# A three-pass attention and expert kernel on one core: GpSimd in place of VectorE for sixteen subtractions

## The reference, cut to what matters

```python
x = x + tanh(g_xattn[0]) * _L0_xattn_ref(..., _layernorm(x), ctx_2048)   # a recurrence (wkv)
x = x + tanh(g_ffn[0]) * _L0_ffn_ref(_layernorm(x), ...)                 # ternary weights, 8-bit tokens
x = x + tanh(g_xattn[1]) * _L1_xattn_ref(_layernorm(x), ctx_2048, ...)   # attention, 32 heads of 8
x = x + tanh(g_ffn[1]) * _L1_ffn_ref(_layernorm(x), ...)                 # 64 experts, top 8, one shared
```

```python
q = _rmsnorm(q)
k = _rmsnorm(k)
scores = jnp.einsum('bhnd,bhmd->bhnm', q, k) * scale
attn = jax.nn.softmax(scores, axis=-1)
```

## Time and profile before

| what | value |
|---|---|
| median of 3 runs | 480.92 us (478.32 to 481.01) |
| the profiled execution's own time | 480.34 us |
| its span in the trace | 478.6 us |
| mean granted TensorE clock | 0.963 of full speed |
| TensorE, matmuls: busy | 399.1 us (83%) |
| VectorE busy | 379.5 us (79%) |
| ScalarE busy | 302.0 us (63%) |
| GpSimd busy | 0.2 us |

### The profile page before, as it was taken

How to read it: one execution, slowest core, us unless ns; L and a number is a source line. 1 busy time by engine, 2 the same in 40 slices (tenths; PEclk the granted TensorE clock), 3 DMA queues, 4 the chain that set the end, 5 groups by cost and what they waited for, 6 DMA issues and landing times.

```text
span 478.6 us, 7806 instructions
## 1 busy us (share of the span) xinstructions
PE 399.1 (83%) x2612; PEld 193.7 (40%) x2612; DVE 379.5 (79%) x817; ACT 302.0 (63%) x442; POOL 0.2 (0%) x4
## 2 busy tenths in 40 slices
PE   1011966697776897999999999999999999999996
PEld 1010444342424454554534443554444444444443
DVE  5999499999998869999797898897456666777754
ACT  5896686689696766757898677464234444444422
POOL 0000000000000000000000000000000000000000
PEclk9999999577898899999999999999999999999999
DMA  8500200000002164114425336244222655556511
GB/s 295 223 1 0 66 1 1 1 1 0 2 2 66 46 213 128 56 57 121 140 72 159 119 111 195 80 143 131 87 66 73 209 164 167 167 172 175 174 38 44
DMA packets 31506, 47.47 MB, mean 99 GB/s; under 512 B 5610, under 2 KB 15210, under 8 KB 30956
## 3 DMA queue, kind: packets, MB, share of 16 engines
q1 hardware_dynamic: 31468, 46.98, 31.4%
HBM read 45.65 MB, written 1.31 MB: 98 GB/s over the span
## 4 chain that ended last, share of the span: by engine, by line
PE 61%; DVE 22%; ACT 7%; issue 4%; DMA 3%; SPq 2%; DVEq 0%; ACTq 0%
PE ps L1593 31%; PE ps L1927 15%; PE ps L1702 5%; PE ps L1690 2%; DVE xn L1034 1%; DVE bn L1015 1%; DMA regC<-in_ctxT_dram 1%; DVE rep L1163 1%; DVE regW L1483 1%; PE ps L1618 1%; DMA regP<-in_dp_dram 1%; PE ps L1584 1%; ACT exs L723 1%; SPq L538 1%; PE ps L1712 1%
## 5 line engine op out<-in xcount | busy, mean ns | idle before, releaser
L934 ACT ACTIVATE regW<-ps 128x512 f32<-128x512 f32 x51 | 30.4, 597 | 92.6 <-PE ps L1593 89.7
L1593 PE MATMUL ps<-hH,regC 128*128 128x512 f16 x264 | 85.8, 380 | 0.1
L1500 DVE TENSOR_TENSOR regW<-ps,regW 128x512 f32<-128x512 f32 x64 | 44.1, 690 | 51.8 <-PE ps L1593 49.0
L1593 PE MATMUL ps<-hH,regW 128*128 128x512 f16 x248 | 80.9, 383 | 0.2 <-DVE regW L1500 0.2
L1593 PE MATMUL ps<-hL,regC 128*128 128x512 f16 x132 | 50.0, 379 | 0.0
L1927 PE MATMUL ps<-regW,regC 128*128 128x512 f16 x198 | 48.1, 379 | 0.0
L1593 PE MATMUL ps<-hL,regW 128*128 128x512 f16 x124 | 47.4, 382 | 0.0
L1927 PE MATMUL ps<-regW 128*128 128x512 f16 x180 | 43.8, 379 | 3.4 <-DVE regW L1483 3.4
L1483 DVE TENSOR_TENSOR regW<-regW 128x512 f16<-128x512 f32 x64 | 43.6, 681 | 0.1
L947 ACT CAST regW<-regW 128x512 f16<-128x512 f32 x64 | 39.2, 612 | 0.6 <-DVE regW L1521 0.5
L1593 PEld LDWEIGHTS ps<-hH,regC 128*128 128x128 f16 x264 | 25.8, 98 | 32.6 <-issue 3.6
(11 more groups left out here) (202 smaller groups left out, 662.1 us busy)
## 6 DMA issues: line engine op xcount, KB each, us to landing
regW<-routing_dram SPq DMA_DIRECT2D x130, 128.0 KB, 3.1
regP<-in_gu_dram SPq DMA_DIRECT2D x56, 256.0 KB, 2.6
regP<-in_dp_dram SPq DMA_DIRECT2D x56, 128.0 KB, 2.7
regO<-in_ffn_dram SPq DMA_DIRECT2D x3, 1024.0 KB, 9.4
x<-in_x_dram SPq DMA_DIRECT2D x2, 512.0 KB, 8.3
regC<-in_ctxT_dram SPq DMA_DIRECT2D x1, 1024.0 KB, 5.3
regP<-in_proj_dram SPq DMA_DIRECT2D x1, 768.0 KB, 12.2
out_dram<-x SPq DMA_DIRECT2D x1, 512.0 KB, 3.5
```

Source lines behind the costliest of these rows:

```text
L934: nc.scalar.activation(sgm[:, c % 2, :], bank(gate_bank(c)), ACT.Silu, scale=UNSCALE).then_inc(esilu_done, 1)
L1500: V.tensor_tensor(rows, bank(gate_bank(c) + 1), rows, ALU.mult).then_inc(et_done, 1)
L1593: mm = T.matmul(out_ap, w(k), a(k), start=(n == 0), stop=(n == 3 * DK - 1))
```

## The change

The function `split_low` moves from VectorE's part of the program to a new part of GpSimd, with the same operands, the same wait and the same semaphore at its end. GpSimd calls it for n = 0 to 15 in a row. On VectorE the ten calls in the plain list and the six in the table of the products are gone, and the calls around them close up. The lists of the other engines are as they were.

```diff
-            (6, "C"): [("ffn_residual", 7, 7), ("split_low", 10), ("split_low", 11), ("stats", 9)],
+            (6, "C"): [("ffn_residual", 7, 7), ("stats", 9)],
...
-            (11, "C"): [("split_low", 12), ("low_halves", 9, 7), ("heads_sum", 16, 6), ("split_low", 13),
-                ("weights_low", 13)],
+            (11, "C"): [("low_halves", 9, 7), ("heads_sum", 16, 6), ("weights_low", 13)],
...
-            (14, "C"): [("split_low", 14), ("split_low", 15), ("weights_low", 16), ("weights_low", 17),
+            (14, "C"): [("weights_low", 16), ("weights_low", 17),
...
-                V.tensor_tensor(lo, src, hi, ALU.subtract).then_inc(repL, 1)
...
+        @block.gpsimd
+        def _(pool):
+            def split_low(n):
+                pool.wait_ge(repH, n + 1)
+                R = rep[:, n % 2]
+                src = kc[:, n % HT, :].rearrange("p (h d) -> p h d", h=HEADS).unsqueeze(2).broadcast_to([P, HEADS, 2, HD])
+                hi, lo = (R[:, :, 0:4:2, :], R[:, :, 1:4:2, :]) if of_keys(n // 2) else (R[:, :, 0:2, :], R[:, :, 2:4, :])
+                nc.gpsimd.tensor_tensor(lo, src, hi, ALU.subtract).then_inc(repL, 1)
+
+
+            for n in range(2 * TT):
+                split_low(n)
```

More of the change, by code:

```diff
@@ L1364, in _ @@
             rows_begin(1)
-            split_low(0)
-            split_low(1)
             rows_end(1)
@@ L1370, in _ @@
             row_sums(2)
-            split_low(2)
-            split_low(3)
             ffn_residual(3, 6)
@@ L1380, in _ @@
             running_max(2)
-            split_low(4)
             low_halves(4, 3)
-            split_low(5)
             turned_rows(4, 1)
@@ L1400, in _ @@
             heads_sum(6, 3)
-            split_low(6)
-            split_low(7)
             heads_sum(7, 2)
@@ L1425, in _ @@
             weights_low(0)
-            split_low(8)
-            split_low(9)
             heads_out(2, 4)
@@ L1459, in beside @@
                         rows(*at)
-                    elif name == "split_low":
-                        split_low(*at)
                     elif name == "stats":
```

## The result

The changed kernel takes 483.13 us (median of 20 runs, 479.39 to 484.7) where the kernel before takes 480.48 us in the same series (20 runs, 478.24 to 482.37). The ratio is 1.0047, with a 95% interval of 1.0029 to 1.0064: half a per cent slower, or 2.3 us. It lies 2.1 us above the forecast of 481.0 and within 0.3 us of rival 1 (483.4). The profiled execution of the changed kernel is the shortest of its 20 runs (479.39 us, span 477.6), so its span says nothing about the 2.3 us. Only its shifts between one place and the next can be read.

What follows compares the result with a forecast made beforehand. From 200 us TensorE was taken to bound the kernel, earlier the hand-overs among VectorE, ScalarE and TensorE. Terms -0.47 + 1.09 - 0.57 = +0.05 us on 480.34 gave 480.4, with 0.6 for the median 481.0; range 478.0 to 487.0.

Steps and rivals of the forecast that it cites:

- rival 1: VectorE and GpSimd hold each other up over SBUF operands, mainly at tiles 4 and 5: +2.4 us, 483.4; chance 0.33.
- The price d: Time of one moved subtraction on GpSimd: taken as 1.22 us, with ends 0.68 and 2.29.
- Term A: Tiles 0 to 3: the second copy of turned tiles ends earlier, -0.47 us.
- Term B: Tiles 6 and 7: TensorE turns tile 7 late and nothing covers it, so the scores come late, +1.09 us.
- Pair (4,5): Tiles 4 and 5: covered by ScalarE's and TensorE's work, earlier gain carried on; no term in the sum.
- term C: Tiles 8 and 9: VectorE, relieved, has the variance 1.2 us earlier, then ScalarE's own queue is late: -0.57 us.
- TensorE's clock: Risk of both signs: a gap in TensorE's work at another place could add or take 2 us.
- Tiles 10 to 15: Beside the products, from 200 us, where TensorE is busy 99.6%: the products cover the move, costed at nothing.

Runs made afterwards that it cites:

- e10: Against the kernel before, only the subtractions of tiles 6 and 7 moved to GpSimd: 481.14 us against 480.54, ratio 1.0012.
- e9: Against the kernel before, only the subtractions of tiles 4 and 5 moved to GpSimd: 482.94 us against 480.35, ratio 1.0057.
- e3: The change with tiles 4 and 5 back on VectorE: 480.16 us against 480.63 for the kernel before, ratio 0.9994.
- e6: Kernel before, nothing moved; GpSimd adds two unneeded two-operand subtractions behind each upper half: 487.36 us against 480.35, ratio 1.0153.
- e7: Kernel before, nothing moved; GpSimd adds two unneeded zero writes behind each upper half: 480.59 us against 480.35, ratio 1.0010.
- e12: The change with TensorE turning tile 5 ahead of group 1's weighted values: 480.94 us against 480.54 for the kernel before, ratio 1.0011.
- e1: The change, all sixteen on GpSimd, with a semaphore of their own: 483.02 us against 480.63 for the kernel before, ratio 1.0040.
- e2: The change with tiles 6 and 7 back on VectorE: 482.46 us against 480.63 for the kernel before, ratio 1.0043.
- e4: Against the kernel before, only tiles 0 to 9 moved to GpSimd: 482.39 us against 480.63, ratio 1.0038.
- e5: Against the kernel before, only tiles 10 to 15 moved to GpSimd: 481.27 us against 480.54, ratio 1.0020.
- e8: The change with tiles 4 to 7 back on VectorE: 479.62 us against 480.35 for the kernel before, ratio 0.9983.
- e11: Against the kernel before, only tiles 0 to 3, 8 and 9 moved to GpSimd: 479.89 us against 480.54, ratio 0.9984.

## Why the prediction was right in its range and wrong in its mechanism

The time lies in the range because the range was drawn wide enough for rival 1, which the forecast itself leaves out. Its own sum is +0.05 us, and +2.3 came.

**The price d: right.** Taken 1.22, measured 1.13 us as half a pair where nothing holds it up. The forecast's condition on it, 0.9 to 1.6, held. The Trainium skill, GPSIMD Engine Reference, section 3.1, whose 1.96 times was weighed against it, is on the dear side here: the shortest single one is 1148 ns, 1.68 times VectorE's 683, and from start to start it is 1.11 us against 0.60, 1.85 times. The page's figure is for 2048 elements of 32 bits. (The prediction's estimate from it should have made the sum +0.5, not +0.6.)

**Term A, pairs (0,1) and (2,3): right.** The second copy ends at 87.30 + 0.69 = 87.99 against 88.22, and 0.21 us of shift comes off on top: -0.44, forecast -0.47. Two errors cancel in it. With d = 1.13 the term is -0.65. But VectorE's small step at 79.35 took 0.44 beside GpSimd's first pair (0.18 at 86.05), and ScalarE's halves at 83.15 are 0.46 later than the 82.69 of the earlier trace rows, of which 0.21 is the old shift: 0.25 late.

**Term B, pair (6,7): right in the trace, not resolved in the time.** Counted from ScalarE's upper halves (117.63, 0.10 earlier than before), the scores are 0.78 + 0.10 = 0.88 later, and ScalarE's wait has grown from 1.77 to 2.65, also 0.88. The working 2d - 1.35 gives 0.91 at the measured d. As time, e10 has +0.6, which an interval of ±1 us can't tell from nothing.

**Pair (4,5): the step that failed.** The prediction called it "covered by ScalarE's and TensorE's work until TensorE comes to it, so the gain is carried on", and gave it no term. For GpSimd's own result that is so: in e9 TensorE doesn't wait for it. What the step puts at nothing is what GpSimd's reading does to VectorE meanwhile. Rival 1 named the place, the instructions and the victim: scans from 91.30, then hL, then the weighted values. All of this came: 2.44 became 4.26, hL began 1.0 us later, TensorE waited 0.72. It is shown from four sides: e3 (gone without this pair), e9 (there with this pair alone), e6 against e7 (two-operand reads without any moved work do it, writes don't) and e12 (the collision stays, TensorE's wait is filled, and by the ratios 1.4 to 1.8 us of the loss go, though the intervals overlap). The forecast had 0.40 and rival 1 had 0.33, both short of certainty, since no row of before had GpSimd at work. The Trainium skill, SBUF — State Buffer, section Who interferes with whom, states that contention, and e6 and e7 bear it out: scans 3.17 beside reads, 2.44 beside writes.

**Rival 1's size: right as a total by luck, not in its parts.** It put TensorE 1.5 us behind the forecast at the weighted values. Measured is 0.8 (e9), and in the change itself 97.24 - 96.69 - 0.21 = 0.34 behind today, which is this 0.8 less the 0.44 of A. The two waits of 1.22 that it supposed for VectorE were 1.82 of stretch. It also took term C away, which the traces below don't bear out. What made up for both is the part that neither it nor the forecast had a term for, TensorE's granted clock.

**TensorE's clock: named as a risk, given no term.** The prediction said that it fails if the clock falls at another place, and that this could be worth 2 us. In e9's trace about 0.9 us come with the stretch from 142 to 147 us, and about 1.7 with the one from 183 to 188: TensorE is 1.13 late at 183.34 (182.21 before) and 2.81 at 188.07 (185.26 before). Between them 0.4 is won back (from 153 to 160 us the clock is 0.76 in e9 and 0.51 in the kernel before), and some 0.3 comes by 182 us without a cause that the rows show. So about 2.2 of this trace's 2.7 us go with the clock.

Over all runs, the five kernels in which the weighted values wait for hL (the change, e1, e2, e4, e9) average 0.960 to 0.962. All others, apart from e6 with its own wait of 2.31 us, average 0.965 to 0.968, and e12 is among these with the same sixteen on GpSimd. So the lower clock goes with the wait. That the wait causes it isn't shown. The traces of e5, e8, e10 and e11, where hL is not late, have a low stretch as well (0.76 from 181 to 188 us), and ahead of both stretches TensorE idles in e9 much as it does before (waits of 0.52 and 0.43 us at 142 in both, and of 3.64 us at 183 against 3.28).

Over the 25 to 35 runs of the kernel before in each series, a run with a mean clock 0.001 lower is 0.11 to 0.16 us longer (correlation -0.77 to -0.82). By that a clock lower by 0.006 to 0.008 would be worth 0.7 to 1.3 us. This is an estimate from runs of another kernel: among the runs of e4 and e9 themselves time doesn't fall with a higher clock (correlation 0.04 and 0.30). How the 0.5 us become 2.3 to 2.7 in the mean of many runs stays open.

**Term C, pair (8,9): right at like clock.** It has to be read between traces with the same clock there. Counted from ScalarE's upper halves of the pair, ScalarE's copies of the turned tiles start, and the root that VectorE's variance feeds starts, after so many us:

| pair (8,9) on | kernel | clock, 142 to 152 us | copies | root |
|---|---|---|---|---|
| VectorE | before | 1.00 | 3.11 | 6.36 |
| VectorE | e9 | 0.83 | 4.21 | 7.28 |
| GpSimd | e3 | 1.00 | 3.48 | 6.24 |
| GpSimd | the change | 0.84 | 4.18 | 6.73 |

At the lower clock the root comes 0.55 earlier with the pair on GpSimd, where -0.57 was forecast, and e1, e4, e8 and e11 (0.83 to 0.85) have 6.74 to 6.78 like the change. The copies are as late with the pair on VectorE as on GpSimd, so it is the clock that delays them. At full clock e3 gains only 0.12: there TensorE waits 0.50 us for GpSimd at tile 9, the cover that the prediction had with 0.2 us to spare. e2, at full clock too, has 5.69. VectorE's instruction on the weights did hold GpSimd in the change, as rival 1 said (1.42 in place of 0.96, the pair 2.99 in place of 2.26), but that did not take the gain away.

**Tiles 10 to 15: forecast nothing, measured about 1 us (e5).** The cover holds in that TensorE is still 99.4% busy from 200 to 300 us, but instructions such as 204.96 and 227.20 last 1.64, 1.65. Where this 1 us would reach the time wasn't found, and e4 against e1 doesn't show it.

The parts measured alone add up to 2.7 (e9) + 0.6 (e10) + 1.0 (e5) - 0.8 (e11), or 3.5 us, against 1.9 (e1) and 2.3 (the change). With about ±1 us on each, they don't contradict one another, which is weak support.

## What to carry to other kernels

Work moved to GpSimd that reads two operands in SBUF is paid twice: in its own longer time, and in the VectorE instructions with two SBUF operands that run beside it. So list what VectorE does in those microseconds before calling the move covered. The price then depends on who waits for the instruction behind the stretched ones. Moving one pair out of eight made the whole loss, and giving TensorE other work at that one wait won most of it back by the medians. And before a shift between two traces is put down to a change, compare TensorE's granted clock in that stretch: here it decided the sign of term C's reading.

## What the runs showed of the hardware that had not been expected

- Both sides are held up, each by up to nearly one instruction of the other: a VectorE instruction of 0.68 us becomes 1.64 (0.96 more, beside subtractions of 1.15), and a subtraction on GpSimd of 1148 ns up to 1869 (0.72 more, beside an instruction of 0.96).
- The subtraction into hL at 228.78, with one operand in PSUM, keeps its 0.68 us in the middle of GpSimd's pair from 226.74 to 229.87, right behind one that was stretched to 1.65.
- A small step with one tensor operand is touched too: 128x64 elements take 0.44 at 79.35 beside GpSimd, and 0.18 at 86.05, as its pair ends.
- GpSimd's writes without reads (e7) cost VectorE nothing: scans 2.44 and subtractions 683 ns, as before.
- Fewer elements read on GpSimd behind every upper half cost more when VectorE keeps its subtractions (e6, 448 for each tile, +7.3 us) than the 512 of the moved ones (+2.3): VectorE's own sixteen stand just there and are held up as well, 912 ns for 683.
- The granted clock of a stretch differs between executions that do the same work there: from 84 to 130 us it is 0.70 in the profiled one of the kernel before and 0.81 in that of e5, which has these subtractions on VectorE as well.
